# Sixteen spare rows, two 64-row tiles for the first projection and two 64-column tiles for the second, in a conv, attention and Fourier kernel

## What is computed

```python
def conv(x):                                      # twice, with other weights
    rw = sigmoid(mean(x, (1, 2)) @ Wr + br)       # routing weights of 4 experts, per image
    h = relu(bn(x @ (rw . Wpw) + rw @ bpw))       # first projection, 24 -> 96 channels
    h = relu(bn(sum_i rw_i * dw3x3_i(h)))         # depthwise 3 x 3, mixed over the experts
    return bn(h @ (rw . Wpwl) + rw @ bpwl) + x    # second projection, 96 -> 24 channels
x = conv1(conv0(x)); t = x as 3136 tokens
t += linear_attention(layer_norm(t))              # 6 heads
t += ffn0(layer_norm(t))                          # operands rounded to an 8-bit float
t += fourier(layer_norm(t))                       # 24 -> 48, FFT over tokens, relu, inverse, 48 -> 24
t += ffn1(layer_norm(t))
```

## Time and profile before

| | us |
|---|---|
| median of 3 runs | 2727.1 |
| lowest and highest | 2726.68, 2732.29 |
| the profiled execution | 2732.07 |
| its span in the trace | 2730.1 |

### The profile page before, as it was taken

One profiled execution on the slowest core, in us unless ns is written; L12 is line 12 of the kernel. 1 busy time (PEld: TensorE's weight loads), 2 busy tenths in 40 slices (PEclk: granted clock), 3 DMA queues, 4 the chain that ended last, 5 costly groups with the idle time before them and its releaser, 6 DMA issues.

```text
span 2730.1 us, 49134 instructions
## 1 busy us (share of the span) xinstructions
PE 2370.9 (87%) x19776; PEld 1324.3 (49%) x19776; DVE 1955.3 (72%) x3878; ACT 1680.7 (62%) x2818; POOL 69.3 (3%) x119
## 2 busy tenths in 40 slices
PE   3867979999898988989898989989899998987866
PEld 1323434564346634664346634665355634663562
DVE  4766778588775977678785978578786887755243
ACT  2324455756756666666756658666776667756644
POOL 1000000000000000000000000000000000000000
PEclk9878888989888988989898998989899998977865
DMA  4001000000001000010001000010000000000000
GB/s 131 1 1 18 1 1 1 11 10 1 18 1 19 2 1 19 2 19 1 13 6 20 1 1 19 2 19 1 1 19 9 2 1 19 2 1 1 19 1 18
DMA packets 108592, 29.43 MB, mean 11 GB/s; under 512 B 104144, under 2 KB 104272, under 8 KB 107984
## 3 DMA queue, kind: packets, MB, share of 16 engines
q1 hardware_dynamic: 108368, 26.29, 4.8%
HBM read 16.64 MB, written 9.63 MB: 10 GB/s over the span
## 4 chain that ended last, share of the span: by engine, by line
PE 61%; DVE 19%; ACT 14%; issue 4%; SPq 1%; DMA 0%; ACTq 0%; POOL 0%; DVEq 0%; POOLq 0%
PE P L666 13%; PE P L647 9%; PE P L711 6%; PE P L681 6%; DVE acc L1347 5%; PE P L856 4%; PE P L687 3%; PE P L702 2%; PE P L869 2%; PE P L897 2%; ACT H L1015 2%; PE P L911 2%; PE P L784 2%; DVE SQ L1482 2%; PE P L725 2%
## 5 line engine op out<-in xcount | busy, mean ns | idle before, releaser
L1347 DVE SCALAR_TENSOR_TENSOR acc<-H,Dm,acc 128x784 f32<-128x784 f32 x1024 | 989.6, 1026 | 189.6 <-ACT acc L1023 189.2
L647 PE MATMUL P<-T,Wk 96*128 96x448 f32 (+1 forms) x768 | 409.3, 618 | 68.4 <-ACT H L1015 51.6
L666 PE MATMUL P<-H,diag 64*64 64x392 f32 x4608 | 409.9, 506 | 5.6 <-DVE T L1363 4.8
L1015 ACT ACTIVATE H<-P,biasA 128x448 f32<-128x448 f32 (+1 forms) x384 | 238.6, 621 | 234.9 <-PE P L647 188.4
L666 PEld LDWEIGHTS P<-H,diag 64*64 64x64 f32 x4608 | 174.3, 137 | 223.3 <-issue 211.3
L711 PE MATMUL P<-T,pack_b 96*96 96x448 f32 x448 | 229.2, 600 | 12.0 <-DVE T L1363 5.8
L647 PEld LDWEIGHTS P<-T,Wk 96*128 96x128 f32 x768 | 137.1, 208 | 180.0 <-ACT H L1015 109.6
L681 PE MATMUL P<-acc,Wk 128*96 128x392 f32 x512 | 202.1, 542 | 25.3 <-ACT acc L1052 25.2
L1046 ACT ACTIVATE acc<-P,biasT 128x392 f32<-128x392 f32 x128 | 68.7, 583 | 228.7 <-PE P L666 228.7
L881 PE MATMUL P<-pack_b,arena 128*96 128x112 f32 x928 | 134.4, 302 | 41.1 <-DVE roots L1482 22.6
L881 PEld LDWEIGHTS P<-pack_b,arena 128*96 128x96 f32 x928 | 116.2, 193 | 72.9 <-DVE roots L1482 32.0
(11 more groups left out here) (186 smaller groups left out, 3886.3 us busy)
## 6 DMA issues: line engine op xcount, KB each, us to landing
xin<-in_x SPq DMA_DIRECT2D x224, 42.0 KB, 2.3
out_y<-arena SPq DMA_DIRECT2D x8, 1176.0 KB, 5.7
pack_b<-in_pack_b SPq DMA_DIRECT2D x1, 3804.0 KB, 17.3
arena<-in_pack_s SPq DMA_DIRECT2D x1, 1444.0 KB, 8.5
pack_a<-in_pack_a SPq DMA_DIRECT2D x1, 1084.0 KB, 5.3
pack_i<-in_pack_i SPq DMA_DIRECT2D x1, 318.0 KB, 3.1
arena<-in_pack_k SPq DMA_DIRECT2D x1, 192.0 KB, 3.2
```

What stands on the lines that cost most here:

```text
L647: pe.matmul(conv_rows(slice(0, 128), H1B, m), Wk1[:, 128 * (u % NT):128 * (u % NT + 1)], image_rows(T[q % 3], a + r0, m), start=True, stop ...
L666: last = pe.matmul(conv_rows(slice(64 * h, 64 * (h + 1)), CVB + r, HH), diag[64 * r:64 * (r + 1), tap, :], H1[64 * r:64 * (r + 1), slot(s, ...
L1015: act.activation(H1[:, slot(s, j), o + r0:o + r0 + m, 1:1 + HW], conv_rows(slice(0, 128), H1B, m), ACT.Relu, bias=biasA[:, j, 1:2]).then_i ...
L1347: ins = ve.scalar_tensor_tensor(a, H1[:, slot(s, j), r:r + SR, c:c + HW], Dm[:, j, tap:tap + 1], a, ALU.mult, ALU.add)
```

## The change

**Rows.** `R` becomes 112: 16 spare rows (`PAD`) stand ahead of the 96, so images 0 and 1 lie in rows 16 to 63 and images 2 and 3 in rows 64 to 111. `RC = 96` is used where the spare rows aren't wanted. The spare rows hold zeros: the transposes read 16 more columns ahead of each block, the weights have zeros there. Transposes with an identity of `R` columns move 112 columns in place of 96 (L784, L961, L983 of the new kernel). The turned Fourier blocks go four to a group in place of five, seven groups in place of six (`NTR`).

**First projection.** Tile 0 reads only rows 0 to 63, tile 2 only rows 64 to 111. The pieces of a strip come in a new order, and the first and the last two stand directly behind each other, one in each 64-row half of the array. Tile 2 uses bank 1, which the taps and the second projection use too; the others stay in bank 0.

```diff
-                for u in range(NU):
-                    a, n, _ = strip_rows(u // NT)
-                    for k, (r0, m) in enumerate(((0, 8), (8, n - 8))):
-                        yield
-                        if u == 0 and k == 0:
-                            pe.wait_ge(cw_ready.sem, cw_ready.at(q, L + 1))
-                        else:
-                            pe.wait_ge(h1_ready.sem, h1_ready.at(q, 2 * (L * NU + u) + k))
-                        pe.matmul(conv_rows(slice(0, 128), H1B, m), Wk1[:, 128 * (u % NT):128 * (u % NT + 1)],
-                                  image_rows(T[q % 3], a + r0, m), start=True, stop=True).then_inc(h1_psum.sem, 1)
+        pieces = ((0, 0), (2, 0), (TJ, 0), (TJ, 1), (0, 1), (2, 1))
+        before_in_bank = (-2, -1, 0, 2, 3, 1)
+                for s in range(NS):
+                    for e, (j, k) in enumerate(pieces):
+                        a, n, _ = piece_rows(s, k)
+                        if j < 2:
+                            yield
+                            if s == 0 and e == 0:
+                                pe.wait_ge(cw_ready.sem, cw_ready.at(q, L + 1))
+                            else:
+                                pe.wait_ge(h1_ready.sem, h1_ready.at(q, NP * (L * NS + s) + before_in_bank[e] + 1))
+                        if j == 2 and k == 0 and s >= 1:
+                            pe.wait_ge(t2_ready.sem, t2_ready.at(q, 2 * (L * NS + s)))
+                        rows = {0: slice(0, 64), TJ: slice(0, R), 2: slice(64, R)}[j]
+                        pe.matmul(conv_rows(slice(0, 128), piece_bank(j), n), Wk1[rows, 128 * j:128 * (j + 1)],
+                                  image_rows(T[q % 3][rows, :], a, n), start=True, stop=True).then_inc(h1_psum.sem, 1)
```

```diff
-                pe.wait_ge(h2_ready.sem, h2_ready.at(q, L * NV + TJ * (s + 1)))
-                for j in range(TJ):
-                    for h in range(2):
-                        pe.matmul(conv_rows(slice(0, R), CVB + h, HH), Wk2[:, j, :], image_rows(acc[:, (NT * s + j) % N2, :], HH * h, HH),
-                                  start=(j == 0), stop=False)
+                pe.wait_ge(h2_ready.sem, h2_ready.at(q, L * NV + 2 * (s + 1)))
+                if s + 1 < NS:
+                    pe.wait_ge(h1_ready.sem, h1_ready.at(q, NP * (L * NS + s + 2)))
                 for r in range(2):
                     for h in range(2):
                         rows = slice(64 * h, 64 * (h + 1))
-                        w = Wk2[rows, TJ, :] if r == h else Wk2t[rows, :]
-                        last = pe.matmul(conv_rows(slice(0, R), CVB + h, HH), w,
-                                         image_rows(acc[rows, (NT * s + TJ) % N2, :], HH * r, HH), start=False, stop=(r == 1))
-                        if r == 1:
-                            last.then_inc(cv_psum.sem, 1)
+                        w = Wk2p[rows, TJ * RC:TJ * RC + R] if r == h else Wk2t[rows, :]
+                        pe.matmul(conv_rows(slice(0, R), CVB + h, HH), w,
+                                  image_rows(acc[rows, (NT * s + TJ) % N2, :], HH * r, HH), start=(r == 0), stop=False)
+                for h in range(2):
+                    for j, out_rows, w in ((0, slice(0, 64), Wk2p[:, 0:64]), (2, slice(64, R), Wk2[:, 2, 2 * CH:RC])):
+                        last = pe.matmul(conv_rows(out_rows, CVB + h, HH), w, image_rows(acc[:, (NT * s + j) % N2, :], HH * h, HH),
+                                         start=False, stop=True)
+                    last.then_inc(cv_psum.sem, 1)
```

```diff
                 for g in groups:
                     n = q * NCK + g
                     if n >= XG:
-                        sp.wait_ge(in_tp.sem, n - XG + 1)
+                        sp.wait_ge(in_tp.sem, n - XG + 2)
...
                 if q == 0:
                     pool_e.wait_ge(setup_late.sem, 1)
+                hold(pool_e, normB.y_ready, normB.y_ready.at(q, 0))
+                pool_e.memset(arena[96:128, reg1:reg1 + TOK], 1.0).then_inc(fpads_set.sem, 1)
+                pool_e.wait_ge(fpads_set.sem, fpads_set.at(q, 1))
+                yield
                 hold(pool_e, out_stored, out_stored.at(q, 16))
...
+                    if n == 2 and c == 0:
+                        act.wait_ge(fpads_set.sem, fpads_set.at(q, 1))
```

347 lines of the change are left out of this document (189 added, 158 removed), and 208 rows, old and new, of the table TURNS.

## The result

The changed kernel takes 2810.7 us (median of 4 runs, 2810.4 to 2816.0) where the kernel before took 2729.5 beside it: ratio 1.030, 95% interval 1.0285 to 1.0316. It is slower by 3%; the forecast was 2640 with a range of 2585 to 2715. The profiled execution took 2810.4, its span 2808.3.

What follows compares the result with a forecast made beforehand. PE's queue was taken to bound the middle. From the profiled 2732.1 us, middle -95, beginning 0 and end +8 gave 2645, or 2640 as the median, since the profiled execution was 5 above it; range 2585 to 2715.

Steps and rivals of the forecast that it cites:

- The tiles' prices: Both projections on PE: halves overlap fully, saving 1.3 us a strip in the second and 1.45 in the first.
- visits: PE going in and out of the array halves: about 0.3 us each, 0.7 us a strip for the new ones.
- forecast 2.05 us: PE's net saving a strip from both projections, 1.3 + 1.45 - 0.7; 115 us over the middle's strips, 126 at its clock.
- no overlap: Rival: the paired tiles on PE go one behind the other and the visits are paid: 2787 us, chance 0.05.
- A term put at nothing: the clock: Middle: the granted clock was taken as it was, 0.91, in the sum.
- First step that failed: Middle: PE's queue sets the pace, so work taken off comes back as time; about a fifth let go, 95 us less.
- Second step that failed: Loop from taps through pieces, second projection and add: 22 us, against about 35 a strip, leaving 13 to spare.
- slower by the loop: Rival: in the middle each hand-over of the bank 1 loop waits behind other work; 2794 us at 1.2 each, chance 0.10.
- The beginning: Convolutions alone: loop gives back at most 1 us a strip, centre taps come later; set at 0, bounds -10 and +10.
- The end: Behind the last convolution: 21 more steps of the quad before, 16 us, half put beside `m`: +8 us.
- The mark I had set: End stretch: if over 350 us, it has taken more back than the forecast gave it.
- The rival of DVE and ACT: Rival: DVE and ACT hold the middle's pace, DVE's share capped at 79%; 2684 us in all, up to 2720, chance 0.18.

Runs made afterwards that it cites:

- run 64: Not a run's label: the words are "Over the whole run 64 strips", meaning the 64 strips of one whole execution of the kernel.
- e2: e1 plus only the column tiles of the second projection, middle tile first, in the old order; 2693 us, ratio 0.983.
- e1: Kernel before with the 16 spare rows alone, both projections whole, pieces all in bank 0, old order; 2707 us, ratio 0.989.
- e6: e2's code with another table of turns from list scheduling and no other difference; 2542 us, ratio 0.929 to the kernel before.
- e8: Changed kernel with ACT's second relu moved behind the next strip's pieces in the first three strips of each convolution; 2880 us, ratio 1.053.
- e9: e5 with the first projection's row tiles undone (pieces whole), banks and waits kept, own table of turns; 2620 us, ratio 0.956.
- e5: Changed kernel's code with another table of turns for PE, ACT and DVE from list scheduling; 2620 us, ratio 0.958.

## Why the prediction was wrong

**The tiles' prices were right.** Second projection: forecast 3.1 us with its visits, measured 2.87. Pair of pieces: forecast 0.75 and some 0.2, measured 0.95. Full overlap of two halves at 392 columns holds. PE's busy time in the middle: forecast about 110 us less, measured 94 less at a lower clock (0.88 for 0.91). Over the whole run 64 strips of the forecast 2.05 us are 131 us, and the work at full clock fell by 133. The rival *no overlap* is out. So is the doubt from the Trainium skill's "TensorE: Matmul & The Clock Gate", Part 3 (an estimate of about 0.78 of the full overlap, from the speedups that it gives for 32-wide tiles): the trace shows none of it for 64-wide ones at 392 columns, where eight rows of L725 take 1.36 us from 1235.98 to the next row, four steps of 0.34.

**A term put at nothing: the clock.** The sum took the clock of the middle as it was. It fell, and 47 of the 133 us came back that way, since PE was busy at the lower level for 615 us in place of 521.

**First step that failed: that PE's queue sets the pace in the middle, so that what leaves it comes back as time.** I took it from 91% busy and 61% of the chain, and let a fifth of the gain go. e2 is that step alone, column tiles on e1 in the old order and nothing else: 58 us less on PE gave 14 us. Three quarters of the gain went, not one fifth. In e6, in an order that suits it, 88 us less on PE (2278 to 2190) gave 53.

**Second step that failed, and the one that gave the sign: the length of the loop and the slack it has.** I wrote 22 us for the loop and about 35 for the strip, 13 to spare. Both were mis-sized. The strip first: 35 was the middle divided by its strips less a guess for routing and input; the period inside a layer in the kernel before is 29.7 us, from the starts of its tap rows. Then the loop. Summed over its links in the changed kernel (means over 48 strips, from the starts and ends of the rows of L702, L1082, L1052, L721, L725 and L1402): taps 6.3; to their emptying 0.1; emptying 1.1; from there until the last piece of the next strip is emptied 14.1; to the second projection 3.4; from its start to the first add 3.7; the add 0.6; to the next taps 1.8. Each link begins where the last one ends, so they add up to the period of 31.1 whatever sets the pace. What shows the loop closed are the small gaps at its hand-overs: taps to emptying 0.1 us, emptying to the piece that waited for it 0.5 (median, 1.3 at most), and the second projection in the median 0.15 us behind the last thing that it waits for, which in 36 of 48 strips is the last piece and in 12 the second relu. The term that was wrong is the pieces: I set four steps of 1.8 and a last relu and centre tap, 8.8 us, read in the beginning where nothing else runs, and it is 14.1 with matmul groups of `m` and `b` in between (the rows at 1218.64 to 1231.45 show how). The 3.4 us until the second projection starts are mostly those 12 strips in which the second relu is late. In the kernel before it started in the median 4 us before the next strip's last piece was emptied. The loop's own length with nothing between its links, 24.7 us (e8) and some 22 at the upper clock level, fits the 22; what I missed is how much stands between its links, and how little of the strip was free.

I had this as the rival *slower by the loop* with a chance of 0.10 and a price of 2794. The mechanism and its direction were right and its chance too low. "The order puts at most a few rows between the steps" was the argument against it; it was false for this table, which puts 17.6 steps of other streams into the stretch from taps to second projection.

**The beginning** was set at 0 with bounds of 10 and is +22. "The strip takes 23.3 now, so the loop gives back at most 1 us" overlooked that DVE's next taps stand in the loop too: the emptying of all pieces stands behind the second relu on ACT, so DVE, which used to go on within 3 to 5 us, waits 9.4. DVE's first tap of the run comes 9 us later (61.1 for 52.1): 4 of them because the first piece itself starts later (50.14 for 46.08), 5 because five emptyings of pieces come ahead of the first centre tap, and not two, as the forecast allowed for. And the clock, 0.81 for 0.89, took what the tiles gave (above).

**The end** was forecast at +8 and is +23: 22 steps more stand behind the last convolution, 21 of them of the quad before the last. PE is busy there for 19 us more (267 for 248), so what they cost found no cover beside `m`. The mark I had set, over 350 us, was met (358).

**The rival of DVE and ACT** had DVE's share capped at 79%. The share was 75% in the middle (1637 of 2171), so PE did stop being the bound, but the cause named was wrong: DVE's wait for centre taps fell to 119 us; what grew were the waits at the loop's links.

**What was never in the sum**: that the change brings a new table of turns, and that a table has a price of its own. The new orders put it at 40 to 80 us here, on top of the 78 for bank 1. (That 78 and 40 make up the 118 us between e2 and the changed kernel is no check: the 40 is worked out as that rest.) How far the waits and how far the table lowered the clock isn't parted by these runs.

## What to carry to other kernels

Before work is taken off the busiest engine, take the distance between two turns of the steady loop from the trace (here 29.7 us a strip), and sum every link of each chain of waits that closes on itself at what the links take where the other streams run, not where they run alone; a new wait that ties the next turn's first step to this turn's middle can cost more than the work it makes room for. Sharing a PSUM bank between two stages turns two loops into one: that cost 78 to 85 us here, while the row tiles that it made possible brought nothing (e9 against e5). And where the order of work is a table, measure a change of code under a table that suits it: the same code was 2811 and 2620 us, and the best of the versions tried was the spare rows and column tiles alone, in a new order, 2542. Look at the granted clock too: work that is taken from an engine which then waits more can come back in part as a lower clock, here 47 of 133 us.

## What the runs showed of the hardware

Two fp32 halves of PE, 64 columns each at 128 rows and 392 columns to stream, run fully at once, as 64-row halves do: 16 rows of both kinds in 2.87 us at the upper clock level. From first start to last end that is 3.04 us, and 5.76 at the lower level.

e1, with matrices of 112 rows, was granted a higher clock than the kernel before with 96. It does no less work (2130 us of PE at full clock for 2110), follows its order and has the same strip period to 0.2 us, and took 2706 to 2715 us at a clock of 0.904 to 0.907 over its four runs, where before took 2729 to 2740 at 0.873 to 0.882 over seven beside it. In the profiled executions (2715 and 2732) PE's busy time is 43 us less and its idle time 26 more (385 for 359), so the gain lies in the clock and not in the waits. The clock is at its upper level (2.4 GHz) or the lower (1.2 GHz) by stretches, and e1 is at the lower for 519 us, the kernel before for 656. Which of its differences does it (the rows, the taps on the middle tile and the second projection that begins with it, the split memset, the input's own spare columns, the seventh turned group) wasn't tried. The rows alone don't fix the clock: the changed kernel has 112 of them and 0.856.
